# Score maxima from four row groups into four banks, a fourth set of probability tiles in two passes, and new engine orders in a four-pass decoder kernel

## What is computed

```python
x = ln(x + attention0(x))                    # pass A ("A1"): 256 keys
x = ln(x + attention0_cross(x, ctx))         # pass B ("A2"): 77 keys
x = ln(x + quantised_mlp(x))                 # pass B ("F")
x = ln(x + attention1_rotary(x))             # pass C ("A3"): 256 keys
x = ln(x + dtw_align(ctx, x))                # distances in C, path between C and D, rest ("E") in D
x = ln(x + attention1_gated(x))              # pass D ("A4"): 256 keys
```

## Time and profile before

| | us |
|---|---|
| runs of before | 6087.66, 6091.51, 6099.28 (median 6091.51) |
| profiled execution, its own time | 6097.69 |
| its span | 6095.9 |
| busy in the span: PE / DVE / ACT / POOL | 5354.1 / 5140.5 / 4107.7 / 2546.5 |
| PE clock granted, mean | 0.967 of full |

### The profile page before, as it was taken

The page is one execution under the profiler, slowest core; times in us unless marked ns, Lnnn a source line. Parts: engine busy times, 40 slices in busy tenths (PEclk is TensorE's granted clock), DMA queues, the critical chain, the costliest instruction groups (busy, mean ns, idle before and its releaser), DMA issues. The chain is left out here.

```text
span 6095.9 us, 142938 instructions
## 1 busy us (share of the span) xinstructions
PE 5354.1 (88%) x54914; PEld 3828.5 (63%) x54914; DVE 5140.5 (84%) x12191; ACT 4107.7 (67%) x7345; POOL 2546.5 (42%) x2574
## 2 busy tenths in 40 slices
PE   6999999879999999969999999998049999999998
PEld 4666666646666666647777777776036666666665
DVE  6888888769999999977777777776859999999997
ACT  5777777658888888866666666665336666666665
POOL 0111111223333333334444444444037677667765
PEclk9999999989999999989999999999569999999999
DMA  1111111110000000010010101010100000000000
GB/s 53 48 43 48 43 48 43 43 32 29 26 28 29 29 29 28 27 41 21 28 33 29 33 29 33 29 32 25 34 22 25 25 29 25 25 25 29 26 25 22
DMA packets 140392, 194.40 MB, mean 32 GB/s; under 512 B 25808, under 2 KB 63696, under 8 KB 139344
## 3 DMA queue, kind: packets, MB, share of 16 engines
q1 hardware_dynamic: 139728, 185.26, 9.7%
HBM read 113.03 MB, written 72.18 MB: 30 GB/s over the span
## 5 line engine op out<-in xcount | busy, mean ns | idle before, releaser
L1008 ACT ACTIVATE Dpr<-pj 128x512 f32<-128x512 f32 x1024 | 528.7, 602 | 255.0 <-PE pj L802 254.6
L1175 DVE TENSOR_REDUCE Amp<-pj 128x2 f32<-128x512 f32 x1024 | 630.9, 685 | 65.0 <-PE pj L869 65.0
L1175 DVE TENSOR_REDUCE Cmp<-pj 128x2 f32<-128x512 f32 x1024 | 638.7, 682 | 49.7 <-PE pj L869 49.7
L1008 ACT ACTIVATE Apr<-pj 128x512 f32<-128x512 f32 x1024 | 522.1, 613 | 205.8 <-PE pj L802 205.8
L1008 ACT ACTIVATE Cpr<-pj 128x512 f32<-128x512 f32 x1024 | 528.8, 602 | 184.6 <-PE pj L802 184.6
L1175 DVE TENSOR_REDUCE Dmp<-pj 128x2 f32<-128x512 f32 x1024 | 644.8, 682 | 9.4 <-PE pj L869 7.2
L1109 POOL TENSOR_SCALAR Ave<-Amv 128x2 f32<-128x2 f32 x64 | 14.7, 229 | 981.2 <-DVE Amv L1242 981.2
L1109 POOL TENSOR_SCALAR Bve<-Bmv 128x2 f32<-128x2 f32 x128 | 29.3, 229 | 870.7 <-DVE Bmv L1242 870.7
L1081 POOL TENSOR_TENSOR Dnrm<-Dnrm,power 128x32 f32<-128x32 f32 x64 | 348.9, 5452 | 98.8 <-DVE Dnrm L1153 98.8
L1116 POOL TENSOR_SCALAR Dx<-Dres,Dmv,Drstd 128x256 f32<-128x256 f32 x256 | 312.6, 1230 | 28.9 <-POOL Drstd L1110 28.9
L1116 POOL TENSOR_SCALAR Bx<-Bres,Bmv,Brstd 128x256 f32<-128x256 f32 x256 | 312.7, 1230 | 28.6 <-POOL Brstd L1110 28.6
(11 more groups left out here) (311 smaller groups left out, 15426.9 us busy)
## 6 DMA issues: line engine op xcount, KB each, us to landing
Ax0T<-in_xT SPq DMA_DIRECT2D x64, 256.0 KB, 2.9
Ax<-in_x SPq DMA_DIRECT2D x64, 256.0 KB, 3.1
x_A_scratch<-Ax SPq DMA_DIRECT2D x64, 256.0 KB, 2.0
Bx<-x_A_scratch SPq DMA_DIRECT2D x64, 256.0 KB, 2.9
x_B_scratch<-Bx SPq DMA_DIRECT2D x64, 256.0 KB, 2.0
Cx<-x_B_scratch SPq DMA_DIRECT2D x64, 256.0 KB, 2.8
x_C_scratch<-Cqr SPq DMA_DIRECT2D x64, 256.0 KB, 2.0
Dx<-x_C_scratch SPq DMA_DIRECT2D x64, 256.0 KB
```

Of the source, the lines that this page charges most:

```text
L1008: ck.tell(act.activation(dst, ck.bank(step + (bank,))[0:n, :], ACT.Exp, scale=HD ** -0.5), "probs_ready", step)
L1175: ins = dve.tensor_reduce(dst, src, AX.X, ALU.max, negate=True)
```

## The change

1. `max_heads` gives a step four heads (B: four pairs), one from each row group; `bank_uses`, `signals` and PE's loops take four banks. In A, C, D a step is 8 matmuls and 4 reduces, a batch has 4 steps; in B 16 matmuls and 4 reduces, 2 steps. The numbers of matmuls and reduces per batch, and their shapes, stay. PE now waits for four free banks before the first matmul of a step.
2. `GROUPS` is 4 in passes A and B (3 stays in C and D).
3. `Clock.wait` issues no wait for a value that this engine's queue has waited for already.
4. All engines' orders in all passes are new.

```diff
-GROUPS = 3
+GROUPS = {"A": 4, "B": 4, "C": 3, "D": 3}
@@ max_heads(att, i)
     if tiles_of(att) == 2:
-        c, e, pair = i // 4, i % 4 // 2, i % 2
-        return [[8 * c + 2 * g + e] for g in (2 * pair, 2 * pair + 1)]
-    return [[2 * g + 1, 2 * g] for g in (2 * i, 2 * i + 1)]
+        c, e = divmod(i, 2)
+        return [[8 * c + 2 * g + e] for g in range(4)]
+    return [[8 * i + 2 * g + 1, 8 * i + 2 * g] for g in range(4)]
@@ max_steps(att)
-    return 4 * tiles_of(att)
+    return 2 * tiles_of(att)
@@ bank_uses(step), kind "max"
-        return [step + (0,), step + (1,)]
+        return [step + (g,) for g in range(4)]
@@ signals, dve
-            "max": ["max_done"] * 2, "shift": ["q_shifted"] * 2,
+            "max": ["max_done"] * 4, "shift": ["q_shifted"] * 2,
@@ Counts (per pass)
-                self.group[step] = len(cores) % GROUPS
-                if len(cores) >= GROUPS:
-                    _, att, b, p = cores[-GROUPS]
+                self.group[step] = len(cores) % groups
+                if len(cores) >= groups:
+                    _, att, b, p = cores[-groups]
@@ Clock.wait
-                    self.eng.wait_ge(sems[name], base[name] + counts.at[step, name, nth])
+                    value = base[name] + counts.at[step, name, nth]
+                    if value > self.reached.get(name, 0):
+                        self.reached[name] = value
+                        self.eng.wait_ge(sems[name], value)
@@ PE, step "max"
-                        for i in range(2):
+                        for i in range(4):
                             ck.wait_bank_free(step + (i,))
                         for hh in range(len(heads[0])):
                             for t in range(QT):
-                                for i in range(2):
+                                for i in range(4):
```

More of the change, by code:

```diff
@@ L127, in before_core @@
     if att == "A1":
-        steps = steps[:2] + maxima(att, b, 0)[:2] + steps[2:] + maxima(att, b, 0)[2:]
+        steps = steps[:2] + maxima(att, b, 0)[:1] + steps[2:] + maxima(att, b, 0)[1:]
     else:
@@ L145, in core @@
     if tiles_of(att) == 2:
-        return p[:1] + second[:2] + p[1:2] + second[2:] + shifted + p[2:3] + first + p[3:] + last
+        return p[:1] + second[:1] + p[1:2] + second[1:] + shifted + p[2:3] + first + p[3:] + last
     return p[:1] + second + shifted + p[1:] + first + last
@@ L186 @@
         "pe": (
-            510, 723, 724, 402, 511, 512, 621, 403, 513, 514, 515, 301, 404, 516, 405, 406, 407, 517, 518,
-            408, 520,
+            3808, 3809, 3917, 3810, 3811, 3919, 3601, 3703, 3812, 3704, 3813, 3814, 3705, 3816, 3602, 3706,
+            3920,
         ),
         "act": (
-            502, 722, 613, 401, 617, 619, 620, 510,
+            3518, 3410, 3201, 3413, 3415, 3416, 3202, 3308,
         ),
         "dve": (
-            514, 515, 404, 516, 405, 406, 407, 725, 408, 623, 624, 411, 412, 303,
+            3912, 3803, 3804, 3805, 3806, 4020, 3809, 4021, 3811, 3919,
         ),
         "pool": (
-            725,
+            21,
         ),
         "sp": (
-            526, 0, 209,
+            2522, 2000, 2107,
         ),
@@ L348, with __init__ @@
 class Counts:
-    def __init__(self, lines):
+    def __init__(self, lines, groups):
         self.at, self.total, self.bank, self.banks = {}, {x: 0 for x in SIGNALS}, {}, [0] * BANKS
@@ L554, in __init__ @@
                 self.ve, self.rstd = each("ve", [P, QT, 2]), each("rstd", [P, QT, 2])
-                self.pr = [[sb(f"{phase}pr{i}_{g}", [P, QT, S], F32, where) for g in range(4)] for i in range(GROUPS)]
+                self.pr = [[sb(f"{phase}pr{i}_{g}", [P, QT, S], F32, where) for g in range(4)] for i in range(GROUPS[phase])]
                 if phase == "A":
@@ L622, in __init__ @@
                 def __init__(self, eng):
-                    self.eng, self.step, self.seen, self.s, self.turn = eng, None, {}, None, None
+                    self.eng, self.step, self.seen, self.s, self.turn, self.reached = eng, None, {}, None, None, {}
                 def move(self, step):
@@ L1377, in _ @@
                                                                          in1=out3[:], op0=ALU.mult, op1=ALU.add))
-                counts = Counts(lines)
+                counts = Counts(lines, GROUPS[phase])
                 with ExitStack() as blocks:
```

39 lines of the change are left out of this document (20 added, 19 removed).

## The result

| | before | after |
|---|---|---|
| median (range), us | 6092.19 (6087.66 to 6099.28) | 6182.81 (6175.58 to 6194.62) |
| span of the profiled execution | 6095.9 | 6192.8 |
| PE clock granted, mean | 0.967 | 0.953 |

The changed kernel takes 1.015 times the time of the one before, 95% interval 1.013 to 1.0169: 90 us slower, where 60 us faster was forecast.

A forecast was written before the change was run, and what follows sets the result against it. DVE was taken to bound passes B and D, PE passes A and C. Terms +30 (A), -27 (C), -9 (B), -56 (D) sum to -62 us: 6097.7 becomes 6036, and 6031 at the median; range 5960 to 6096.

The forecast's parts named there:

- DVE's list is the same work in another order. I find no DVE wait in it.: Pass B: reordering leaves DVE's work unchanged and without waits; round 22.22 against 22.36, -9 us.
- +30: Pass A: stalls of PE lengthen the round from 17.94 to 18.4 us, 30 us over 64 rounds.
- the dropped waits: All passes: not repeating satisfied waits gains nothing, or 0.05 us before each core's first exponential; -13 to 0, taken as 0.
- my 22.9: Pass C: round of 22.9 us against 23.41, work 21.6 plus remaining stalls; -33, with drain +6, -27 us.
- The wait just vanishes: Pass D: 8.3 us of DVE work covers the 8.2 us load chain; round 23.45 against 24.33, -56 us.
- the 1.2 us kind: Pass D: gate estimated at 1.7 us, five small DVE operations, one of them of 1.2 us.
- DVE's floor: Pass D: DVE can't go under 24.33 - 0.9 = 23.4 us a round, whatever PE does.
- (a): Rival, slower: four banks at once cost 2.5 us of stalls a round in every 256-key pass; 6152 us, chance 0.12.
- (b): Rival, about no change: POOL late by 1 us keeps D's DMA wait, D gains nothing; 6086 us, chance 0.13.
- (c): Rival, better in A: stalls overlap more, round 17.2 us, -47 us instead of +30; 5954 us, chance 0.15.
- (d): Rival: the maxima don't run four abreast, +0.9 us a round in A and C, +113; 6144 us, chance 0.05.
- if DVE in D waits for the DMA as before: Pass D: sign that would prove the forecast wrong; it expected no DVE wait and DVE over 95% busy.

The follow-up runs named there:

- e13: Changed kernel with POOL's residual base in pass B written as four instructions of 128x128 instead of one of 128x512; 6077.7 us, 0.9961 of the kernel before.
- e5: Changed kernel with ln(F) behind norm.1 and shift.1 behind ln(A2) in B's DVE list, SP's store in B one round later; 6048.1 us, ratio 0.9926.
- e10: Kernel before with pass A alone changed (order, four heads and four banks a step, four groups), repeated waits kept; 6137.4 us, ratio 1.0057.
- e15: Changed kernel with A and B as before and SP's stores of C and D one round later; 5973.8 us, 0.9801 of the kernel before.
- e12: Kernel before with only a fourth group of probability tiles in A and B and the repeated waits dropped; 6085.3 us, ratio 0.9971.
- e8: Changed kernel with SP's store of pass D one round later, nothing else; 6167.6 us, 1.0121 of the kernel before.
- e14: Changed kernel with POOL's residual base and feed-forward layer norm in pass B each cut into four instructions of 128x128; 6054.1 us, ratio 0.9918.
- e1: Changed kernel with the four transposes of pass B's second normalisation done four times over; 6134.5 us, 1.0049 of the kernel before.

## Why the prediction was right or wrong

- **B, wrong, the step that failed:** "DVE's list is the same work in another order. I find no DVE wait in it." The same operations aren't the same durations. I carried their times over from rows in which POOL was elsewhere, and laid POOL's list under none of the passes. The new list puts `fq` under POOL's layer norms: +1.5 us. That delay makes DVE late at `max.0`, whose banks the ring of eight hands to the gate; PE idles, its clock halves in 27 of 44 rounds, and `shift.0` comes late: +0.97 more. e13 shows that the first causes the second. There was indeed no wait, and e5 gives 22.32 against my 22.22 once both are away.
- **A, right in size and in layout, in part by luck:** 18.45 against 18.4, +29 us against +30. PE's steps start within 0.2 us of where I laid them, for instance `pv.1` 1.8 us behind `core.0` (1.9), `norm.0` 5.5 (5.7), `core.2` 10.4 (10.5), `k` 15.7 (15.6), counted from 613.63 and 595.19 us in the timeline. But two errors cancel in it: the order with its four-bank steps costs 0.74 (18.68 in e10), and the dropped waits, which I took as nothing, give back 0.23.
- **C, right in direction, a term left out:** 23.20 against 22.9. The order laid out by hand does give 22.83 (e15), but I asked of the load of x only in B and D: in C it stands on SP behind the store of the distances, and half of the rounds wait for it, 0.37 us on the mean. And 0.27 of the 0.6 that e15 gains in C is what the dropped waits give the kernel before (e12), so that my 22.9 was partly luck: no run has C's new order with the repeated waits kept. The bound I gave those waits, 0.05 us ahead of the exponentials, was too small: PE's idle behind `max` and `core`, 0.60 in the earlier trace rows, is 0.45 in e12, once ahead of `pv` and once ahead of `norm` in a round. C also starts 19 us later behind B; with the old B that is 2.5.
- **D, the right number by a wrong step, which is luck:** 23.33 against 23.45. "The wait just vanishes": it grew, from 0.9 to 1.2 us a round. One round of the changed kernel, whose statistics of `ln(A4)` end at 5020.36: the end of `gate`, and `path`:

```profile
5027.42 0.16 DVE L1307 TENSOR_TENSOR Dlg<-Dlg,Dgs 128x4 f32<-128x4 f32 x1
5029.81 0.35 DVE L1217 TENSOR_SCALAR Dkb<-twice,Dends 77x256 f32<-77x256 f32 x1 [2.23 <-DMA Dx<-x_C_scratch]
```

  DVE's work from 5020.27 to the end of `gate` took 7.3 us, not 8.3: `gate` took 0.8 and not 1.7, since its operation of 1.2 us was no longer under POOL. The chain took 9.4 in this round, against 8.2 in the earlier trace rows; in the median round of either kernel the part behind POOL's `x` takes 4.3, so what let the wait grow on the mean is mostly the shorter work. What paid instead are two collisions with POOL: L1301 had a mean of 992 ns and has 191, L1324 had 1095 and has 213 (stretch 4700 to 5800; L1305 and L1328 in the changed kernel). DVE's busy time fell from 22.6 to 20.8 us a round. I had even used "the 1.2 us kind" of small operation as a duration without asking why 128x30 should take 1.2 us. I took 24.33 less the wait as DVE's floor; e8, at 22.96, is under it.
- **The rivals:** none held. (a) had the sign, by stalls in C and D that didn't come: C's round is 22.83 with four banks once its load is there. Its price for C was also off by its own terms: 2.5 against 1.25 us of stalls is 1.25 a round and not 0.9, so 6174 and not 6152. (Two smaller slips: a `core`-`max` pair stalls PE by 1.96 less 0.96 and 0.32, that is 0.68 and not 0.6 us, and 6036 less 6 is 6030.) (b) was right that D's load wait stays, but that didn't cost D its gain. (c) and (d) are out: A's round was as laid out. None of the four had B in it.
- **What would show it wrong** was named rightly for D ("if DVE in D waits for the DMA as before"), and it happened, though D's time came out.

## What to carry to other kernels

When an order changes, lay DVE's and POOL's lists under each other, not only against PE: an oddly long duration of a tiny operation can be a wait in disguise, as here, and it moves with the order. Where POOL's work must lie beside DVE's, shorter POOL instructions can help, as in e13 and e14. Ask of every idle time of PE also what it does to the clock, and of every moved statistic or layer norm which store waits for it and which load is queued behind that store.

## What was not expected of the hardware

- PE's idle stretch of 1.71 us stood in every round of B, and in 27 of 44 its clock halved, for some 6 us in the round shown; DVE waited for that. With 1.41 us on the mean (e13) it fell in 2 of 48 rounds, with 12 extra transposes ahead of the gap (e1) in none. Those 12 transposes a round saved some 62 us.
- A DVE operation on 128x2 took 1195 ns beside a POOL instruction of 1.27 us and 381 ns when that was cut in four; `fq`'s reduce in the same stretch kept its length (679 ns against 674).
- Waits that were satisfied already cost 0.15 us ahead of `pv` and again ahead of `norm` in each round of C; e12, which drops them and adds the fourth set of tiles in A and B, was 0.3% faster. In A's round of the kernel before they cost nothing that shows (17.92 against 17.94).
